# Scores of four attention layers from float32r parts instead of bf16 parts, with two heads on row tiles of the array

## The chip, the cores and the metric

The kernel runs on one core of one Trainium2 chip. The metric is the device time of one execution in microseconds, lower is better. Times of engines and queues come from one profiled execution.

## The reference, cut to what matters

Four layers follow each other on one batch of 2048 tokens of width 256. Each layer is a cross attention against a context of 1601 rows of width 192, and a mixture of experts:

```python
for L in range(4):
    x = x + xattn[L](layernorm(x), ctx_768)     # 2048 x 256 against 1601 x 192
    x = x + ffn[L](layernorm(x))                # 16, 8, 8, 16 experts

def xattn(x, y):                                # 16 heads of 16; layer 2: 8 heads of 32
    q, k, v = x @ Wq + bq, y @ Wk + bk, y @ Wv + bv
    att = softmax(q @ k.T / sqrt(dh))           # layer 3: masked keys, no biases
    return (att @ v) @ Wo + bo
```

All of it is float32. The softmax subtracts the exact maximum of each row.

## The kernel before, in words

The programs of the engines are written out by hand, one block an engine, with semaphores between them. Each layer has the stages normalisation, projections, attention, routing and experts, with a fence of all five engines between two stages. The change touches the first three.

**Normalisation.** Meanwhile POOL clears `v` and writes its columns of ones (L645, L646), then joins the fence. In layer 0 a fence stands ahead of this, which SP joins after it has issued the loads of `x`, the context, the mask (L410, L412, L414) and the weights.

**Projections.** 16 tiles of 128 x 512, first the keys and then the queries. TensorE forms a tile (L1476 to L1480), ScalarE copies it twice out of PSUM (`qk` as f32, `qk_part` as bf16, L771 and L773), VectorE forms the second and the third bf16 part of what is left (L1007 to L1009), and SP stores three parts to DRAM (L433). A head's product q k is then six products of parts. SP loads the keys back as `k_stack` (L371): six parts of 16 rows one below the other, 16 heads, all 1601 keys, and under them four constant rows (L360) for the mask and for the maximum. In layer 2 (heads of 32 rows) six parts don't fit in 96 rows, so each head has two such stacks (`nsub` = 2), and every score or maximum is two matmuls that accumulate.

**Attention.** Four iterations of 512 queries, each of four groups of 4 heads (layer 2: 2 heads), each group of 13 slots of 128 keys. Iterations 1 and 2 are a loop. In one slot TensorE issues, in this order:
- side jobs, taken from a list that `side_schedule` spreads over the 13 slots: two ahead of the scores, the others between them;
- `scores` of the slot for each head: keys as weights, 512 queries as the moving operand (L1566). Two heads fill a pair of banks; there are two pairs, banks 0 to 3;
- `weigh` of the slot before: v as weights of 32 (64) columns on a column tile for each head, the exponentials as moving operand, two instructions each, accumulated in bank 4 over the 13 slots (L1580).

ScalarE takes the exponential of a pair of banks in one instruction (L797), in layer 3 with the mask as bias. The side jobs use banks 5 to 7 in turn. TensorE waits for VectorE to have finished the job three back. The jobs are:
- `max`: 128 queries against 401 or 400 keys of a head of the next group, or the one after it (L1536), of which VectorE takes the row maximum (L1028). 64 of them make a group's maxima (layer 2: 32, each of two matmuls);
- `turn`: the maxima transposed (L1539), negated and split in three bf16 parts by VectorE (L1035 to L1040), stored and loaded as rows 97 to 99 of `q_stack` by SP (L399, L404). The scores of that group wait for them;
- `den`, `spread`: the denominators are picked out (L1542), inverted (L1046), widened by ScalarE, transposed (L1546), and applied by VectorE (L1051);
- `out`: four times in an iteration, eight f32 matmuls with Wo (L1551), added to x (L1057). All four fall in the first group.

In a prologue ahead of the loop, group 0 and three eighths of group 1 get their maxima, 88 jobs. SP loads the queries of the next groups (L384) as `weigh` frees their buffers.

TensorE's order within a slot, and the two waits that pace it:

```python
for job in slot[:2]: side(job)
for j in range(npair):
    for i in range(2):
        scores(g, k, j, i)          # i == 0 waits for the exponentials of two pairs back
        for job in slot[cut[2*j+i]:cut[2*j+i+1]]: side(job)   # waits for VectorE, three jobs back
weigh(g, k - 1)
```

## Time and profile before

| | |
|---|---|
| median of 3 runs (lowest, highest) | 4534.62 us (4534.21, 4538.73) |
| profiled execution: span from the first to the last instruction | 4547.7 us |
| instructions | 61161 |
| TensorE matmul busy | 3983.5 us, 88% |
| TensorE weight load busy | 1804.0 us, 40% |
| VectorE busy | 2670.7 us, 59% |
| ScalarE busy | 1975.0 us, 43% |
| GpSimd busy | 207.4 us, 5% |
| mean granted TensorE clock | 0.915 of full speed |

The page gives the span of the profiled execution and no other time for it. Busy time is the union of an engine's instructions. Matmuls overlap each other, so the mean duration of one is longer than the distance between two. PEld is TensorE's weight load, which runs beside its matmuls.

### The profile page before, as it was taken

How to read it: one execution, taken by the hardware profiler on the slowest of the kernel's cores; microseconds unless marked ns; L12 is line 12 of the kernel's file. 1: busy time of each engine (PE TensorE's matmuls, PEld its weight loads, DVE VectorE, ACT ScalarE, POOL GpSimd, SP SyncE). 2: the span in 40 equal slices, each digit the busy share in tenths (PEclk: the TensorE clock that was granted, in tenths of full speed). 3: DMA queues.
4: the chain of work that ended last, by engine and by line, in shares of the span. 5: the costliest groups of instructions: out<-in, count | busy, mean ns of one | idle time of the engine just before them, and what ended most of it. 6: DMA issues, size and time to landing. Idle time of an engine off the chain costs nothing. (4 is left out here: it accounts for less than half of the span.)

```text
span 4547.7 us, 61161 instructions
## 1 busy us (share of the span) xinstructions
PE 3983.5 (88%) x19174; PEld 1804.0 (40%) x19175; DVE 2670.7 (59%) x5907; ACT 1975.0 (43%) x2374; POOL 207.4 (5%) x420
## 2 busy tenths in 40 slices
PE   4999999699599999947994799999786999997894
PEld 2233333466323333335663234443441333333463
DVE  3888786445488878632224554443456887883322
ACT  2476677222247667712332243334012766765110
POOL 1000000000000000021003000000000000001202
PEclk8799999899779999958997899999795999997897
DMA  7000000000600000042113200000023000001144
GB/s 135 15 12 13 10 12 2 18 18 18 101 12 12 13 10 12 2 161 102 31 31 90 64 12 12 11 9 1 23 47 67 12 13 9 12 5 66 49 146 111
DMA packets 131231, 170.84 MB, mean 38 GB/s; under 512 B 30119, under 2 KB 111215, under 8 KB 128914
## 3 DMA queue, kind: packets, MB, share of 16 engines
q1 hardware_dynamic: 121362, 136.37, 12.2%
q0 software_dynamic: 9600, 31.04, 2.3%
q8 instruction: 149, 2.44, 0.2%
q14 instruction: 120, 0.98, 0.1%
HBM read 114.12 MB, written 54.66 MB: 37 GB/s over the span
## 5 line engine op out<-in xcount | busy, mean ns | idle before, releaser
L1028 DVE TENSOR_REDUCE mx<-ps 128x1 f32<-128x400 f32 (+1 forms) x3584 | 1809.8, 565 | 538.7 <-PE ps L1536 533.9
L797 ACT ACTIVATE probs<-ps,zero_col 128x1024 f32<-128x1024 f32 (+1 forms) x1040 | 1111.7, 1110 | 741.0 <-PE ps L1566 740.6
L1536 PE MATMUL ps<-k_stack,q_stack 97*128 97x400 bf16 (+3 forms) x4096 | 1233.1, 352 | 142.9 <-DMA q_stack<-ones_row 120.7
L1566 PE MATMUL ps<-q_stack,k_stack 100*128 100x512 bf16 (+2 forms) x3328 | 1080.9, 383 | 4.1 <-ACT probs L797 3.9
L1580 PE MATMUL ps<-probs,v 128*32 128x512 f32 (+2 forms) x5824 | 896.9, 611 | 0.2 <-ACT probs L797 0.2
L1536 PEld LDWEIGHTS ps<-k_stack,q_stack 97*128 97x128 bf16 (+1 forms) x4096 | 343.7, 98 | 1255.2 <-DVE mx L1028 703.6
L797 ACT ACTIVATE probs<-ps,mask_col 128x1024 f32<-128x1024 f32 (+1 forms) x416 | 440.3, 1110 | 188.1 <-PE ps L1566 187.9
L1566 PEld LDWEIGHTS ps<-q_stack,k_stack 100*128 100x128 bf16 (+2 forms) x3328 | 325.0, 100 | 321.5 <-ACT probs L797 59.1
L1283 DVE SCALAR_TENSOR_TENSOR x_res<-ps,comb,x_res 128x256 f32<-128x256 f32 x336 | 149.1, 483 | 154.5 <-PE ps L1710 154.1
L1580 PEld LDWEIGHTS ps<-probs,v 128*32 128x32 f32 (+2 forms) x5824 | 140.3, 112 | 234.1 <-issue 223.2
L1695 PE MATMUL ps<-xn_t,w_up 128*128 128x512 f32 (+1 forms) x416 | 192.8, 603 | 34.1 <-DVE comb L1182 22.6
L1448 PE MATMUL ps<-ident,xn 128*128 128x128 f32 x256 | 51.6, 383 | 146.7 <-DVE xn L984 109.5
L1710 PE MATMUL ps<-w_down,h_t 128*128 128x256 f32 x736 | 170.2, 380 | 4.0 <-ACT h_t L892 4.0
L1710 PEld LDWEIGHTS ps<-w_down,h_t 128*128 128x128 f32 x736 | 138.9, 190 | 53.5 <-issue 37.4
L1774 PE MATMUL ps<-w_all,xn_t 128*128 x624 | 144.6, 385 | 3.8 <-ACT xn_t L861 2.4
L1753 PE MATMUL ps<-w_all,xn_t 128*128 x312 | 142.4, 599 | 0.4 <-issue 0.4
L1007 DVE TENSOR_TENSOR qk_rest<-qk,qk_part 128x512 f32<-128x512 f32 x64 | 40.5, 633 | 172.0 <-ACT qk_part L771 128.4
L1551 PE MATMUL ps<-wo,o_t 128*128 128x256 f32 x512 | 131.1, 405 | 11.0 <-DVE mx L1028 7.6
L1774 PEld LDWEIGHTS ps<-w_all,xn_t 128*128 128x128 f32 x624 | 118.2, 192 | 43.0 <-issue 28.4
L861 ACT ACTIVATE xn_t<-ps,tile_bias 128x128 f32<-128x128 f32 x312 | 84.7, 382 | 99.7 <-PE ps L1765 99.4
L892 ACT ACTIVATE h_t<-ps 128x512 f32<-128x512 f32 x80 | 46.7, 596 | 177.0 <-PE ps L1695 176.9
L1695 PEld LDWEIGHTS ps<-xn_t,w_up 128*128 128x128 f32 (+1 forms) x416 | 79.6, 192 | 110.5 <-issue 95.1
(205 smaller groups left out, 2664.4 us busy)
## 6 DMA issues: line engine op xcount, KB each, us to landing
q_stack<-q_parts SPq DMA_DIRECT2D x384, 64.0 KB, 2.3
k_stack<-k_parts SPq DMA_DIRECT2D x48, 400.2 KB, 12.2
q_parts<-qk_part SPq DMA_DIRECT2D x32, 384.0 KB, 10.1
w_up<-in_up SPq DMA_DIRECT2D x17, 704.0 KB, 4.4
x_place<-zeros POOLq DMA_DIRECT2D x2, 5120.0 KB, 26.5
k_parts<-qk_part SPq DMA_DIRECT2D x24, 384.0 KB, 5.8
w_all<-in_up SPq DMA_DIRECT2D x5, 1024.0 KB, 16.4
w_all<-in_down SPq DMA_DIRECT2D x5, 1024.0 KB, 19.8
```

Source lines behind the costliest of these rows:

```text
L797: act.activation(PR[pair[0] % 4][0:r, :, :], PS[0:r, 2 * b:2 * b + 2, :], ACT.Exp, bias=mask_col[0:r, k:k + 1] if L == 3 else zero_col[0:r ...
L861: last = act.activation(HB[:, q * P:(q + 1) * P], PS[:, 2 + q // 4, q % 4 * P:(q % 4 + 1) * P], ACT.Gelu, bias=BT[:, bass.ds(i, 1), q], sc ...
L1028: ins = dve.reduce_max(MX4[g % 2][:, u, c:c + 1], PS[:, bank, 0:CK[c]], AX.X)
L1283: dve.scalar_tensor_tensor(X[:, t, :], PS[:, b, 0:D], c, X[:, t, :], ALU.mult, ALU.add).then_inc(s_yf, 1)
L1536: last = mm(PS[:, bank, 0:CK[c]], QS[g][0:rows, s, qt * P:(qt + 1) * P], KS[0:rows, ks0, CKO[c]:CKO[c] + CK[c]], start=sub == 0, stop=sub ...
L1551: last = mm(PS[:, bank, 0:D], OT[:, g, i * P:(i + 1) * P], WO[:, g, :], start=g == 0, stop=g == NG - 1)
L1566: last = mm(PS[0:r, b + i, :], KS[0:rows, (g * hpg + jj) * nsub + sub, k * P:k * P + r], QS[g][0:rows, slot_of(jj) + sub, :], start=sub == ...
L1580: last = mm(PS[pw * jj:pw * jj + pw, 4, :], V[0:r, k, (g * hpg + jj) * pw:(g * hpg + jj) * pw + pw], PR[used[0] % 4][0:r, i, :], start=k = ...
L1695: last = mm(PS[0:rows, b, :], up[:, k, off + at:off + at + rows], xnT[:, k, c * Q:(c + 1) * Q], start=k == 0, stop=k == 1)
L1710: last = mm(PS[:, b, 0:D], HT[(c - 1) % 2][0:rows, t, i * P:(i + 1) * P], WD[par][0:rows, t, :], start=t == 0, stop=t == len(ft) - 1)
L1753: last = mm(PS[:, half, :], XT1[par][:, k * P:(k + 1) * P], w1.rearrange("p a f -> p (a f)"), start=k == 0, stop=k == 1)
L1774: last = mm(PS[:, 4 + par, 0:D], HB[:, q * P:(q + 1) * P], w2.rearrange("p a f -> p (a f)"), start=q == 0, stop=q == NF // P - 1)
```

## The change

The six bf16 products become three products of float32r parts: q and k are each kept as two f32 words of which TensorE reads the leading part (float32r), stored in DRAM and in SBUF as 4 bytes. A head of 16 rows now takes 3 x 16 + 3 = 51 rows, so two heads stand one above the other, on rows 0 to 63 and 64 to 127 of the array (`hps` = 2); a head of 32 takes 99 rows in one piece (`hps` = 1, no second matmul). The mask goes in as a row of `k_stack` in layer 3, and the maximum as two rows. The constant rows come from clearing the whole of `k_stack` to 1 and of `q_stack` to 0 (1 in layer 3) on POOL, ahead of the fence that ends normalisation. A score tile is now one bank (banks 0 to 2 in turn) with an exponential of its own; the sums are in bank 3. A maximum job covers two heads, in two banks at a time (4 and 5, or 6 and 7), with one VectorE instruction for both; TensorE waits for the job two back. No side job stands ahead of a slot's first score any more. Matmuls of the maxima are issued so that the row halves alternate. The mask columns, their loads and the bias of the exponentials are gone.

```diff
-CK = [401, 400, 400, 400]
+CK = [402, 400, 400, 400]
-ATT = [dict(dh=16, pw=32, hpg=4, nsub=1), dict(dh=16, pw=32, hpg=4, nsub=1),
-       dict(dh=32, pw=64, hpg=2, nsub=2), dict(dh=16, pw=32, hpg=4, nsub=1)]
+ATT = [dict(dh=16, pw=32, hpg=4, hps=2), dict(dh=16, pw=32, hpg=4, hps=2),
+       dict(dh=32, pw=64, hpg=2, hps=1), dict(dh=16, pw=32, hpg=4, hps=2)]
+Q_PART, K_PART = [0, 0, 1], [0, 1, 0]
...
-    units = hpg * TPQ
+    units = hpg // 2 * TPQ
...
-    jobs = late + early[:6] + ([("turn", (g + 1) % NG)] if nxt1 else []) + early[6:]
+    jobs = late + early[:3] + ([("turn", (g + 1) % NG)] if nxt1 else []) + early[3:]
...
-            KS = sb("k_stack", [100, 16, S], bf16, att)
+            KS = sb("k_stack", [P, 8, S], f32r, att)
-            PR = [sb(f"probs{i}", [P, 2, Q], f32, att) for i in range(4)]
-            QS = [sb(f"q_stack{i}", [100, 4, Q], bf16, att) for i in range(4)]
+            QS = [sb(f"q_stack{i}", [P, 2, Q], f32r, att) for i in range(4)]
+            PR = [sb(f"probs{i}", [P, Q], f32, att) for i in range(8)]
...
-            QP = [sb(f"qk_part{i}", [P, 3, Q], bf16, prj) for i in range(4)]
+            QP = [sb(f"qk_part{i}", [P, 2, Q], f32r, prj) for i in range(4)]
...  SP
-                load_constant_rows(L)
+                if L == 3:
+                    load_mask_rows(L)
...
+                keys = k_parts[K_PART[third]].rearrange("(s i d) n -> i d s n", i=hps, d=dh)
+                for i in range(hps):
+                    row = 64 * i + third * dh
+                    sp.dma_start(KS[row:row + dh, half * 4:half * 4 + 4, :].bitcast(f32),
+                                 keys[i][:, half * 4:half * 4 + 4, :]).then_inc(s_ks, 16)
...
+                for third in range(3):
+                    queries = q_parts[Q_PART[third]].rearrange("(s i d) t -> i d s t", i=hps, d=dh)
+                    for i in range(hps):
+                        row = 64 * i + third * dh
+                        sp.dma_start(QS[buf][row:row + dh, :, :].bitcast(f32),
+                                     queries[i][:, 2 * g:2 * g + 2, bass.ts(c, Q)]).then_inc(s_ql[buf], 16)
-                sp.dma_start(dst[96:97, :, :], ones_row[:]).then_inc(s_ql[buf], 16)
...
-            sp.dma_start(mask_u8[:, 0:NK - 1], A["mask"][:, 0:P * (NK - 1)].rearrange("a (k p) -> p (a k)", p=P),
-                         allow_slow_non_contiguous=True).then_inc(s_in, 16)
-            sp.dma_start(mask_u8[0:KREM, NK - 1:NK], A["mask"][:, P * (NK - 1):S].rearrange("a p -> p a"),
-                         allow_slow_non_contiguous=True).then_inc(s_in, 16)
...  POOL
+                for buf in QS:
+                    link(pool.memset(buf[:].bitcast(f32), 1.0 if L == 3 else 0.0))
+                link(pool.memset(KS[:].bitcast(f32), 1.0))
                 fence(pool, fences)
-                link(pool.memset(MP[:, 0, :], 0.0))
...  ACT
-                    for j in range(npair):
-                        b = pair[0] % 2
+                    for j in range(hpg):
                         sc.step()
                         act.wait_ge(s_sc, sc.at())
-                        if pv.n > 3:
-                            act.wait_ge(s_pv, pv.at(3))
-                        pv.step()
-                        act.activation(PR[pair[0] % 4][0:r, :, :], PS[0:r, 2 * b:2 * b + 2, :], ACT.Exp,
-                                       bias=mask_col[0:r, k:k + 1] if L == 3 else zero_col[0:r, :],
-                                       scale=1.0).then_inc(s_pr, 1)
+                        if j % 2 == 0:
+                            if pv.n > 3:
+                                act.wait_ge(s_pv, pv.at(3))
+                            pv.step()
+                        act.activation(PR[tile[0] % 8][0:r, :], PS[0:r, tile[0] % 3, :], ACT.Exp).then_inc(s_pr, 1)
...  DVE
-                    link(dve.tensor_tensor(r, x, p[:, 0, 0:n], ALU.subtract))
-                    link(dve.tensor_copy(p[:, 1, 0:n], r))
-                    dve.tensor_tensor(p[:, 2, 0:n], r, p[:, 1, 0:n], ALU.subtract).then_inc(s_pp, 1)
+                    dve.tensor_tensor(p[:, 1, 0:n], x, p[:, 0, 0:n].bitcast(f32), ALU.subtract).then_inc(s_pp, 1)
...
-                    bank = 5 + njob[0] % 3
+                    bank = 4 + 2 * (njob[0] % 2)
...
-                        ins = dve.reduce_max(MX4[g % 2][:, u, c:c + 1], PS[:, bank, 0:CK[c]], AX.X)
+                        lo = u // TPQ * 2 * TPQ + u % TPQ
+                        dve.reduce_max(MX4[g % 2][:, lo:lo + TPQ + 1:TPQ, c], PS[:, bank:bank + 2, 0:CK[c]], AX.X)\
+                            .then_inc(s_sf, 1)
...
-                        link(dve.tensor_copy(MP[0:units, 1, :], neg))
-                        link(dve.tensor_tensor(rest, neg, MP[0:units, 1, :], ALU.subtract))
-                        link(dve.tensor_copy(MP[0:units, 2, :], rest))
-                        dve.tensor_tensor(MP[0:units, 3, :], rest, MP[0:units, 2, :], ALU.subtract).then_inc(s_mp, 1)
+                        link(dve.tensor_copy(MP[0:units, 0, :], neg))
+                        dve.tensor_tensor(MP[0:units, 1, :], neg, MP[0:units, 0, :].bitcast(f32), ALU.subtract)\
+                            .then_inc(s_mp, 1)
...  PE
+                def place_of(j):
+                    return 64 * (j % hps), j // hps
...
-                        if sf.n > 2:
-                            pe.wait_ge(s_sf, sf.at(2))
+                        if sf.n > 1:
+                            pe.wait_ge(s_sf, sf.at(1))
...
-                        for sub in range(nsub):
-                            rows = 97 if sub == 0 else 96
-                            s = slot_of(j) + sub
-                            ks0 = (g * hpg + j) * nsub + sub
-                            last = mm(PS[:, bank, 0:CK[c]], QS[g][0:rows, s, qt * P:(qt + 1) * P],
-                                      KS[0:rows, ks0, CKO[c]:CKO[c] + CK[c]], start=sub == 0, stop=sub == nsub - 1)
+                        for i in (high, 1 - high):
+                            row, s = place_of(u // TPQ * 2 + i)
+                            end = row + 3 * dh + 1
+                            last = mm(PS[:, bank + i, 0:CK[c]], QS[g][row:end, s, qt * P:(qt + 1) * P],
+                                      KS[row:end, 2 * g + s, CKO[c]:CKO[c] + CK[c]], start=True, stop=True)
...
+                def scores(g, k, j):
                     r = key_rows(k)
+                    if tile[0] == 0:
+                        if pr.n > 0:
+                            pe.wait_ge(s_pr, pr.at())
+                    elif tile[0] > 2:
+                        pe.wait_ge(s_pr, pr.at(2))
+                    pr.step()
+                    row, s = place_of(j)
+                    end = row + 3 * dh + 3
+                    mm(PS[0:r, tile[0] % 3, :], KS[row:end, 2 * g + s, k * P:k * P + r], QS[g][row:end, s, :],
+                       start=True, stop=True).then_inc(s_sc, 1)
+                    tile[0] += 1
...
-                            for job in slot[:2]:
-                                side(job)
-                            cut = [2 + n for n in chunk_of(max(len(slot) - 2, 0), 2 * npair)]
-                            for j in range(npair):
-                                for i in range(2):
-                                    scores(g, k, j, i)
-                                    for job in slot[cut[2 * j + i]:cut[2 * j + i + 1]]:
-                                        side(job)
+                            cut = chunk_of(len(slot), hpg)
+                            for j in range(hpg):
+                                scores(g, k, j)
+                                for job in slot[cut[j]:cut[j + 1]]:
+                                    side(job, 1 - j % 2)
```

## Rows read from the trace of the kernel before

**Rows 1.** Windows: prologue and main loop of layer 0, main loop of layer 2.
```profile
core 0: us, PE busy (x) PEld busy (x) DVE busy (x) ACT busy (x) POOL busy (x), PEclk, DMA share, GB/s
114.70:160.60 45.90, 42.64 (x91) 9.50 (x92) 43.97 (x95) 0.00 (x0) 0.00 (x0) 0.50 0.10 26
160.60:802.00 641.40, 632.22 (x3693) 223.02 (x3692) 511.03 (x1080) 452.10 (x443) 0.00 (x0) 0.99 0.03 9
...
2541.00:3168.00 627.00, 623.06 (x2909) 243.87 (x2910) 306.56 (x637) 245.85 (x237) 0.00 (x0) 0.99 0.03 10
```

**Rows 2.** Timeline, a slot of layer 3: start, length, engine, line, count, wait.
```profile
3560.30 1.07 PE L1580 MATMUL ps<-probs,v 128*32 128x512 f32 x8
...
3561.30 0.51 PE L1536 MATMUL ps<-k_stack,q_stack 97*128 97x400 bf16 x2
...
3561.64 0.60 PE L1566 MATMUL ps<-q_stack,k_stack 100*128 100x512 bf16 x2
3561.68 2.50 DVE L1028 TENSOR_REDUCE mx<-ps 128x1 f32<-128x400 f32 x5 [0.33 <-PE ps L1536]
...
3562.08 0.33 PE L1536 MATMUL ps<-k_stack,q_stack 97*128 97x400 bf16 x1
...
3562.28 2.12 ACT L797 ACTIVATE probs<-ps,mask_col 128x1024 f32<-128x1024 f32 x2 [0.71 <-PE ps L1566]
...
3563.12 1.07 PE L1580 MATMUL ps<-probs,v 128*32 128x512 f32 x8
```

**Rows 3.** Chain of waits, layer 3: start, length, what.
```profile
3454.38 30.90 DVE mx L1028 x64
...
3547.24 1.03 PE ps L1542 x8
...
3586.34 1.02 PE ps L1542 x8
...
3677.85 1.91 PE ps L1551 x8
...
3827.47 1.86 PE ps L1580 x8
...
3850.03 1.92 PE ps L1551 x8
...
4015.14 1.97 PE ps L1551 x8
```

**Rows 4.** Timeline, layer 2, two successive `weigh` blocks.
```profile
2602.96 1.08 PE L1580 MATMUL ps<-probs,v 128*64 128x512 f32 x4
...
2605.63 1.08 PE L1580 MATMUL ps<-probs,v 128*64 128x512 f32 x4
```

**Rows 5.** Groups by form: count, busy us, mean ns, idle before.
```profile
L1028 DVE TENSOR_REDUCE mx<-ps 128x1 f32<-128x400 f32 x2688 | 1408.8, 565 | 362.4 <-PE ps L1536 360.4
...
L1695 PE MATMUL ps<-xn_t,w_up 128*128 128x512 f32 x384 | 179.3, 604 | 34.1 <-DVE comb L1182 22.6 <-DVEq L1227 11.4
...
L1331 DVE COPY xn_t<-ps 128x512 f32<-128x512 f32 x78 | 53.9, 691 | 94.0 <-PE ps L1753 94.0
...
L741 ACT ACTIVATE xn_t<-ps 128x512 f32<-128x512 f32 x64 | 34.5, 596 | 79.3 <-PE ps L1448 79.2
...
L1339 DVE COPY xn_t<-ps 128x256 f32<-128x256 f32 x39 | 16.6, 424 | 119.4 <-PE ps L1774 119.4
```

**Rows 6.** Timeline, end of layer 1's loop, ScalarE back to back.
```profile
1931.51 4.16 ACT L797 ACTIVATE probs<-ps,zero_col 128x1024 f32<-128x1024 f32 x4 [0.19 <-PE ps L1566]
```

**Rows 7.** Timeline of POOL, normalisation of layer 1.
```profile
1153.94 5.64 POOL L645 MEMSET v<- 128x6656 f32 x1 [317.04 <-SPq L318]
...
1169.96 0.19 POOL L648 MEMSET m_part<- 16x128 bf16 x1 [9.87 <-ACTq L318]
```

**Rows 8.** Timeline of SP's queue at the start.
```profile
4.59 3.66 SPq L412 DMA_DIRECT2D mask_u<-in_mask  x1
```

**Rows 9.** Windows of the projections of layer 1, columns as in rows 1.
```profile
1172.00:1176.00 4.00, 4.00 (x14) 2.46 (x13) 2.12 (x4) 2.72 (x6) 0.00 (x0) 1.00 0.88 26
...
1236.00:1240.00 4.00, 0.00 (x0) 0.00 (x0) 0.83 (x2) 1.26 (x2) 0.00 (x0) 0.50 0.94 324
```

More of the change, by code:

```diff
@@ L831, in _ @@
                     n = NG * NK * npair
[L832 removed]
+                    for c, per in ((sc, 2 * n), (pv, n), (o, n), (ot, NG), (rd, NG), (dv, NG)):
                         c.loop(it, 1, per)
@@ L1079, in _ @@
                 with dve.Fori(1, NQ - 1) as it:
-                    loops = ((sj, per), (sf, per), (md, 64), (v, 4 * 3), (rx, NG))
+                    loops = ((sj, per), (sf, per), (md, 64), (v, 4), (rx, NG))
                     for c, p in loops:
@@ L1553, in side @@
                     last.then_inc(s_sj, 1)
-                def scores(g, k, j, i):
+                def scores(g, k, j):
                     r = key_rows(k)
-                    b = 2 * (pair[0] % 2)
-                    if i == 0:
-                        if pr.n > 1:
-                            pe.wait_ge(s_pr, pr.at(1))
-                        pr.step()
-                    jj = 2 * j + i
-                    for sub in range(nsub):
-                        rows = 100 if sub == 0 else 96
-                        last = mm(PS[0:r, b + i, :], KS[0:rows, (g * hpg + jj) * nsub + sub, k * P:k * P + r],
-                                  QS[g][0:rows, slot_of(jj) + sub, :], start=sub == 0, stop=sub == nsub - 1)
-                    if i == 1:
-                        pair[0] += 1
-                        last.then_inc(s_sc, 1)
+                    if tile[0] == 0:
[8 more added lines that the diff above has]
+                       start=True, stop=True).then_inc(s_sc, 1)
+                    tile[0] += 1
                 def weigh(g, k):
```

137 lines of the change are left out of this document (51 added, 86 removed).

## The prediction

> **What bounds the kernel now.** I looked first at the windows of the stages [rows 1]. The main loop of attention in layer 0 takes 641 us and that of layer 2 627 us; layers 1 and 3 run the loop of layer 0 again, so four such loops are over half of the 4547.7 us span. TensorE is busy for 632 of the 641 us at clock 0.99, VectorE for 511, ScalarE for 452. A busy engine need not be the limit, so the timeline of one key slot comes next [rows 2]. From one start of the eight `weigh` matmuls (L1580) to the next it is 2.82 us (3560.30 to 3563.12), and TensorE has no hole in it: `weigh` 1.00 us, then five maxima matmuls (L1536) 0.17 us apart (two of them from 3561.30 to 3561.64) and four score matmuls (L1566) 0.22 us apart (two from 3561.64 to 3562.08), 5 x 0.17 + 4 x 0.22 = 1.73 us, and about 0.1 us where the kind of matmul changes. VectorE's five maxima take 2.50 us, ScalarE's two exponentials 2.12 us. TensorE ends last, VectorE 0.3 us behind it. The chain of waits [rows 3] gives the pace of a whole group (13 slots, 64 maxima): the eight `den` matmuls (L1542) are 39.1 us apart, 13 x 2.82 = 36.7 plus den, spread and turn. An iteration of four groups is 172.2 or 165.1 us from `out` to `out` (L1551), so the group that holds the four `out` jobs is 48 to 55 us; I take 51. Layer 2 has half the exponentials and is bound by TensorE alone: 2.67 us between its `weigh` blocks [rows 4].
>
> **TensorE, layers 0, 1 and 3.** Matmuls per slot stay at 4 scores and 64/13 = 4.92 maxima, each now on 51 or fewer rows of one half of the array, the halves alternating. No row shows float32r or two row halves at work together. Bounds: at best two at a time at today's column rate, 1.71 / 2 = 0.85 us per slot; at worst no overlap, 1.71 us. (4 x 0.215 + 4.92 x 0.172 = 1.71.) What may come between is the weight load, since four-byte weights load slower: the `den` matmuls, four columns behind 128 f32 weights each, are 1.03 / 8 = 0.129 us apart [rows 3]. 8.92 x 0.129 = 1.15 us. I take 1.15, because the `weigh` matmuls, eight f32 ones on four column tiles, already finish in 1.00 us, where eight on the whole array at 0.467 us (L1695, 179.3 us busy for 384 [rows 5]) would take 3.7: this array does overlap tiles. With 1.00 for `weigh` and 0.1 for the changes of kind a slot is 2.25 us of TensorE, a group 29.3 + 2 (den, spread, turn) = 31.2, the `out` group 7.7 more (4 x 1.92 [rows 3]) = 38.9.
> The row shows 0.1 us per slot lost between kinds of matmul, no more [rows 2]. The Trainium skill ("TensorEngine Tiling (Array Packing)", Tiling Modes) says that a change of tiling mode drains the engine. By that rule den, spread, turn and out, which now stand between row-tiled matmuls, would add some ten changes a group, 1 us; it would alter only the `out` groups, by 10 us in all.
>
> **VectorE.** 64 maxima of 400 columns become 32 of 800. 64 of them back to back take 30.90 us in the prologue, 0.483 us each [rows 3], against a duration of 0.565 [rows 5]. A copy goes from 0.424 to 0.691 us for 256 columns more [rows 5], 1.04 ns a column. So 800 columns cost 0.483 + 400 x 1.04 ns = 0.90 us; the bounds are 0.90 and 2 x 0.483 = 0.97. A group is 32 x 0.90 = 28.8 us, and the other jobs (reciprocal, spread, turn, final reduce with their waits for TensorE) about 3.3: 32.1 us. VectorE becomes the bound of an ordinary group. 33 jobs over 13 slots are six slots of two and seven of three. In a slot of two VectorE needs 1.8 us and TensorE 8 x 0.129 + 1.1 = 2.1, so 6 x 0.3 = 1.8 us may be lost, with two pairs of banks where three single ones stood: 32.1 to 33.9 us, and I take 33.5. The `out` group stays with TensorE: 38.9 plus the 3 us by which today's exceeds its own sum (36.7 + 2 + 7.7 = 46.4 against 48 to 55), 42 us.
>
> **ScalarE.** Two activations of 1024 columns become four of 512. Four of the long ones back to back take 4.16 us [rows 6], 1.02 apart against a duration of 1.11; a short one lasts 0.60 [rows 5], so 0.51 apart: 2.04 us a slot both ways. If the 0.09 us did not overlap it would be 2.4, still under 2.58 (33.5 / 13). Cost nothing while VectorE covers it. A score waits for the exponential three tiles back, and three tiles are 1.5 us of ScalarE's work against 1.0 us of `weigh`.
>
> **Sum for layers 0, 1, 3.** Of 16 groups 11 are ordinary and full, 11 x (39.1 - 33.5) = 62 us; three have `out`, 3 x (51 - 42) = 27, of which I count 24; one has five eighths of the maxima (4); the last has none and is ScalarE's (1). 91 us a layer, **-273**.
>
> **Layer 2.** 99 rows hold all three products, so scores fall from 4 to 2 matmuls a slot and maxima from 4.92 to 2.46, untiled. 1.71 becomes 0.85 us if float32r streams as bf16 does, and TensorE stays the bound (VectorE 1.23 x 0.90 + 0.25 = 1.4, ScalarE 1.0). 0.85 x 13 = 11 us a group, some 170 us; I take off 20 for an overhead per four-byte matmul like that of L1695 (0.467 us against twice the 0.213 us that 512 columns take at 2.4 GHz: 0.04): **-150**.
>
> **The rest.** The prologue is VectorE's: 44 x 0.90 = 39.6 against 88 x 0.483 = 42.5, -3 a layer, **-12**. The two new clears on POOL, 4 x 1024 columns of `q_stack` and 12808 of `k_stack`, stand before the fence that ends normalisation. `v`'s 6656 columns take 5.64 us [rows 7], so they cost 14.9 us. POOL now ends 9.9 us before that fence (L645, L646, then idle until 1169.96), so the fence comes 5 us later in each layer. In layer 0 the longer of the two removed mask loads gives SP 3.7 us back ahead of the first fence [rows 8], leaving 1. Together **+17**. In the projections the four constant rows go, whose broadcasts keep the DMA engines 0.88 busy at only 26 GB/s as the projections begin [rows 9], some 5 us, and the stored parts grow from 384 to 512 KB a tile, 1.8 MB a layer, 5.5 us at the 324 GB/s at which the last stores drain [rows 9]. I count **0**, with 10 us a layer either way. TensorE now has pauses, and its clock may fall at times, as it is 0.50 in the prologue, where it waits for VectorE [rows 1]. I add **+25**.
>
> -273 - 150 - 12 + 17 + 25 = -393 us from the 4547.7 us span: 4155. The page gives no other time for that execution; the median of the runs, 4534.6, is 13.1 us less than its span, so the forecast is **4142 us**. Its own range is 4050 to 4250: 32.1 us a group is -55, 35 us +60, the projections and clears 40 either way.
>
> **Rivals.** (1) *The halves do not overlap*, or the waits between them keep them apart. TensorE's slot stays 2.82 us, and only layer 2 gains (and no pauses cost clock): 4547.7 - 150 - 12 + 17 - 13 = **4390**. For it: nothing here shows row tiles. Against: column tiles overlap. Chance 0.13.
> (2) *The clock falls*, the case that ends slower. It decides in the main loops of layers 0, 1, 3, where TensorE would wait for VectorE some 0.3 us of each slot. At 0.5 clock `weigh` takes 1.86 us [rows 3] and the pairs 1.67 by columns, 3.7 us a slot, 1.15 more than my 2.58. Over 46 groups that is 690 us if it lasts, and it outweighs the gain from 57% of the time on; at all times about 4830. At 30% of the time it is 4350. For it: the prologue runs at 0.50 with TensorE shown busy for 42.6 of 45.9 us [rows 1]. Against: at half clock TensorE has no pause, and today that brings the clock back as soon as the main loop starts. 0.06 for a part of it, 0.04 for slower.
> (3) *float32r takes the passes of f32.* f32 needs two instructions of 0.467 us for 512 columns [rows 5]. Overlapped in pairs, layers 0, 1, 3: (4 x 0.93 + 4.92 x 0.73) / 2 + 1.1 = 4.8 us a slot; layer 2 the same without overlap: about 6000 us. With one such instruction instead of two the slot is 2.9 everywhere, some 80 us slower than before. 0.05 together.
> (4) *The parts hold up but VectorE gains nothing* (0.97 a job, all coupling lost): 36.5 us a group, 4240. Within 0.72 for the forecast.
>
> **Numbers.** Forecast and (4) 0.72, (1) 0.13, part of (2) 0.06, slower 0.09. A measurement of this kernel tells about 0.2%, 9 us, from no change. Faster 0.90, same 0.01, slower 0.09. The range 4050 to 4395 takes in (1) and most of (2).
>
> **What would show it.** L1028 at half the count and 0.97 to 1.0 us each; den to den 33 to 34 us in layer 3; alternate L1566-like matmuls starting 0.13 us apart or less; VectorE's waits for TensorE small and TensorE's for VectorE large; layer 2's slot near 2.0 us with two score matmuls 0.22 us apart; the fence after normalisation 5 us later; granted clock above 0.95 in all four main loops. Wrong: matmuls in alternate halves 0.2 us apart, a float32r duration near 0.6 us, or clock 0.5 inside the loops.

## The result: slower by 6%, and the profile after

The changed kernel takes 4811.5 us (median of four runs, 4792.3 to 4842.8) against 4535.9 us before (4534.2 to 4538.7), a ratio of 1.0616 with an interval of 1.0571 to 1.0661. The forecast was 4142 us. The profiled execution has a span of 4840.7 us, 293 us over the one of before. From its page: the span, the busy times, and the granted clock in 40 slices.

```profile
span 4840.7 us, 58262 instructions
...
PE 4026.7 (83%) x18246; PEld 2014.0 (42%) x18247; DVE 2522.0 (52%) x3854; ACT 1953.7 (40%) x3830; POOL 262.3 (5%) x434
...
PEclk8698888699969989965998698888885988995797
```

The windows of attention in the four layers, each from its first exponential to its last, before and then after (the columns as in [rows 1], whose windows are cut a little otherwise):

```profile
163.10:806.30 643.20, 633.87 (x3712) 222.98 (x3710) 509.18 (x1077) 454.97 (x446) 0.00 (x0) 0.99 0.03 9
1297.20:1940.00 642.80, 633.49 (x3712) 222.81 (x3710) 509.46 (x1077) 455.04 (x446) 0.00 (x0) 0.99 0.04 9
2557.60:3171.60 614.00, 612.86 (x2876) 239.82 (x2873) 293.89 (x609) 246.81 (x239) 0.00 (x0) 1.00 0.03 9
3502.20:4146.70 644.50, 634.97 (x3712) 223.16 (x3710) 509.49 (x1077) 455.20 (x447) 0.00 (x0) 0.99 0.04 9
```
```profile
163.90:911.60 747.70, 689.02 (x3707) 283.82 (x3710) 481.59 (x582) 447.11 (x862) 0.00 (x0) 0.86 0.03 8
1414.80:2148.60 733.80, 671.42 (x3707) 275.12 (x3710) 481.47 (x582) 447.25 (x862) 0.00 (x0) 0.88 0.03 8
2775.80:3356.70 580.90, 544.07 (x2003) 260.02 (x2002) 265.19 (x350) 248.41 (x447) 0.00 (x0) 0.87 0.03 9
3687.20:4435.50 748.30, 690.43 (x3709) 281.93 (x3710) 481.70 (x582) 447.59 (x863) 0.00 (x0) 0.86 0.03 8
```

Layers 0, 1 and 3 lose 105, 91 and 104 us, and layer 2 gains 33. That is +267 of the 293 us. Two things changed: TensorE had at most 10 us of holes in a layer and now has 37 to 62 us, and its granted clock fell from 0.99 to between 0.86 and 0.88. The costliest groups by line say what ends the holes (busy time and mean ns of one, then idle time before them and what ended it):

```profile
L1005 DVE TENSOR_REDUCE mx<-ps 128x2 f32<-128x800 f32 (+1 forms) x1792 | 1710.0, 988 | 832.1 <-PE ps L1511 827.5
L782 ACT ACTIVATE probs<-ps 128x512 f32<-128x512 f32 (+1 forms) x2912 | 1527.9, 600 | 1175.4 <-PE ps L1541 1168.5 <-issue 5.4
...
L1511 PEld LDWEIGHTS ps<-k_stack,q_stack 49*128 49x128 f32 (+1 forms) x3584 | 518.2, 214 | 378.5 <-DVE mx L1005 236.1 <-issue 122.0 <-DVE m_neg L1012 0.9
L1541 PEld LDWEIGHTS ps<-q_stack,k_stack 51*128 51x128 f32 (+2 forms) x2912 | 462.8, 204 | 1222.8 <-ACT probs L782 752.4 <-issue 402.9 <-DMA q_stack<-m_parts 39.1
```

VectorE and ScalarE wait for TensorE, and TensorE's weight loads wait for both of them: a ring, in which no engine is full. The timeline of one slot of layer 1 at granted clock 1.00 shows it (start, duration, engine and line, and in brackets the idle time and its releaser):

```profile
1530.15 0.50 PE L1541 MATMUL ps<-q_stack,k_stack 51*128 51x512 f32 x2
...
1530.66 0.40 PE L1541 MATMUL ps<-q_stack,k_stack 51*128 51x512 f32 x1
1530.68 2.06 ACT L782 ACTIVATE probs<-ps 128x512 f32<-128x512 f32 x4 [1.08 <-PE ps L1541]
1530.87 1.00 DVE L1005 TENSOR_REDUCE mx<-ps 128x2 f32<-128x804 f32 x1 [0.50 <-PE ps L1511]
...
1531.33 0.49 PE L1541 MATMUL ps<-q_stack,k_stack 51*128 51x512 f32 x1 [0.27 <-ACT probs L782]
...
1531.33 0.67 PE L1511 MATMUL ps<-k_stack,q_stack 49*128 49x400 f32 x2
...
1531.93 1.06 PE L1553 MATMUL ps<-probs,v 128*32 128x512 f32 x8
1532.04 0.99 DVE L1005 TENSOR_REDUCE mx<-ps 128x2 f32<-128x800 f32 x1 [0.17 <-PE ps L1511]
...
1532.93 0.50 PE L1541 MATMUL ps<-q_stack,k_stack 51*128 51x512 f32 x2
...
1533.46 1.58 ACT L782 ACTIVATE probs<-ps 128x512 f32<-128x512 f32 x3 [0.71 <-PE ps L1541]
```

The two scores at 1530.15 start and end together, 0.50 us for both, where two took 0.60 us before [rows 2]: the halves do overlap. But the fourth score finds all three score banks taken and waits for the first exponential (1530.68 + 0.60). `weigh` stands behind that score, and ScalarE, done at 1532.74, gets its next tile only 0.5 us after `weigh` ends. In series: score 0.5, exponential 0.6, fourth score and maxima 0.6, `weigh` 1.0, some 2.8 us (here 2.78; more in a slot of three maxima jobs). The mean slot at clock 1.00 is 3.12 us, against 2.93 before, both counted as said below.

### The profile page after: what moved, and what is told of

Read it like the earlier page. It is cut to its first block and busy times, and to the rows that moved or that the text cites. A ratio compares the mean times of both kernels' runs of the same rounds, so it can differ in the third digit from the quotient of the medians.

```text
span 4840.7 us, 58262 instructions
## 1 busy us (share of the span) xinstructions
PE 4026.7 (83%) x18246; PEld 2014.0 (42%) x18247; DVE 2522.0 (52%) x3854; ACT 1953.7 (40%) x3830; POOL 262.3 (5%) x434
## 5 line engine op out<-in xcount | busy, mean ns | idle before, releaser
L1005 DVE TENSOR_REDUCE mx<-ps 128x2 f32<-128x800 f32 (+1 forms) x1792 | 1710.0, 988 | 832.1 <-PE ps L1511 827.5
L782 ACT ACTIVATE probs<-ps 128x512 f32<-128x512 f32 (+1 forms) x2912 | 1527.9, 600 | 1175.4 <-PE ps L1541 1168.5
L1541 PE MATMUL ps<-q_stack,k_stack 51*128 51x512 f32 (+2 forms) x2912 | 1146.7, 517 | 147.6 <-ACT probs L782 94.0
L1511 PE MATMUL ps<-k_stack,q_stack 49*128 49x400 f32 (+3 forms) x3584 | 924.1, 428 | 191.3 <-DMA q_stack<-q_parts 115.9
L1553 PE MATMUL ps<-probs,v 128*32 128x512 f32 (+2 forms) x5824 | 1033.6, 699 | 0.0
L1541 PEld LDWEIGHTS ps<-q_stack,k_stack 51*128 51x128 f32 (+2 forms) x2912 | 462.8, 204 | 1222.8 <-ACT probs L782 752.4
L1511 PEld LDWEIGHTS ps<-k_stack,q_stack 49*128 49x128 f32 (+1 forms) x3584 | 518.2, 214 | 378.5 <-DVE mx L1005 236.1
L985 DVE TENSOR_TENSOR qk_part<-qk,qk_part 128x512 fp32r<-128x512 f32 x64 | 39.9, 633 | 232.3 <-ACT qk_part L757 162.4
L1424 PEld LDWEIGHTS ps<-ident,xn 128*128 128x128 f32 x256 | 49.7, 218 | 196.1 <-issue 102.9
```

The lines of the kernel that those rows point to most:

```text
L782: act.activation(PR[tile[0] % 8][0:r, :], PS[0:r, tile[0] % 3, :], ACT.Exp).then_inc(s_pr, 1)
L1005: dve.reduce_max(MX4[g % 2][:, lo:lo + TPQ + 1:TPQ, c], PS[:, bank:bank + 2, 0:CK[c]], AX.X)\
L1424: last = pe.transpose(PS[:, 2 * (c % 2) + half, i * P:(i + 1) * P], XN[:, c * TPQ + i, half * P:(half + 1) * P], ident[:])
L1511: last = mm(PS[:, bank + i, 0:CK[c]], QS[g][row:end, s, qt * P:(qt + 1) * P], KS[row:end, 2 * g + s, CKO[c]:CKO[c] + CK[c]], start=True, s ...
L1541: mm(PS[0:r, tile[0] % 3, :], KS[row:end, 2 * g + s, k * P:k * P + r], QS[g][row:end, s, :], start=True, stop=True).then_inc(s_sc, 1)
L1553: last = mm(PS[pw * jj:pw * jj + pw, 3, :], V[0:r, k, (g * hpg + jj) * pw:(g * hpg + jj) * pw + pw], PR[used[0] % 8][0:r, :], start=k == 0 ...
```

## The experiments

"A slot" below is the mean distance from the first exponential of one slot to that of the next, in layers 0, 1 and 3, over the slots that run at clock 1.00 from end to end, without the groups that hold the `out` jobs. Each comes from the run's one profiled execution. The edits are cut to the lines that matter.

### The order in the changed kernel

**e1_weigh_before_last.** In slots of four heads, `weigh` goes ahead of the last score.
```diff
-    for j in range(hpg): scores(g, k, j); ...
-    weigh(g, k - 1)
+    for j in range(hpg):
+        if j == hpg - 1 and hpg == 4: weigh(g, k - 1)
+        scores(g, k, j); ...
```


> The changed kernel, but in the layers with four heads a group TensorE issues the weigh matmuls ahead of the slot's last score instead of behind it. Theory chain: with three score banks the last score of a slot waits for the exponential of the slot's first score, and weigh stands behind it, so score latency 0.5, exponential 0.6, last score and maxima 0.6 and weigh 1.0 follow one another (2.8 to 3.0 us a slot at full clock). With weigh moved ahead of that wait the slot falls to 2.4 to 2.6 us, den to den in layers 1 and 3 at full clock from 41 to 33 to 36 us, and the total to 4250 to 4450 us, the clock rising above 0.93 as TensorE has fewer holes. Rival clock: the loss is the lower clock alone, set by what the matmuls are (half of the rows), so the slot at full clock changes little and the total stays within 1.5% of the changed kernel's 4812. Rival no overlap: the row halves do not work together and TensorE's own work fills the slot: no change beyond 1%.

4718.1 us, ratio 1.0398 (1.0362 to 1.0433), 94 us less. The exponential's wait is real, and a third of the loss. The slot falls from 3.12 to 2.98 us only, not to the 2.4 to 2.6 expected, so something else holds it as well.

**e3_same_half.** The second maximum of a pair no longer starts in the half that the last score left free.
```diff
-    side(job, 1 - j % 2)
+    side(job, j % 2)
```


> The changed kernel with the order of each maxima pair turned round, so that a maxima matmul follows a score on the same row half instead of the other one. If halves overlap, the matmuls that follow on the same half are 0.17 to 0.22 us apart and those that change half 0.10 to 0.13. Theory chain: in total under 1.5% slower, since the slot's length is waits. Rival no overlap: no difference in the distances at all.

4839.7 us in one run at clock 0.843, slot 3.11 us: no difference from the changed kernel that one run can tell.

**e4_half_maxima.** The maxima read 200 of each 400 columns; the rest is left out.
```diff
-    PS[:, bank:bank + 2, 0:CK[c]]
+    PS[:, bank:bank + 2, 0:CK[c] // 2]
```


> The changed kernel, but VectorE's maxima read half of the columns of each bank (the other half of the keys is left out of the maxima), so one lasts about 0.57 us instead of 0.99. Theory chain: VectorE is not what the slot waits for, the total falls by less than 2% (some 0.1 us a slot where a maxima pair waits for it). Rival VectorE with only two pairs of banks as the bound: the slot falls by about 0.4 us per job, 0.5 to 1 us a slot, 300 us or more in total.

4541.4 us in one run, 270 less, at clock 0.879, slot 2.93 us. That was far more than the theory of an exponential chain alone allowed: the wait for VectorE is the larger one.

**e6_early_weigh_half_maxima.** Both edits.

> The changed kernel with the weigh ahead of the last score (e1) and maxima that read half of their columns (e4); the other half of the columns is left out of the maxima. Theory (two waits in series in each slot, VectorE's and the exponential's): the gains add, -94 and -270 us on 4811, about 4450 us, and a slot at full clock is 2.3 to 2.4 us. Rival (one wait only, each edit shortens the same one): no better than e4 alone, 4520 to 4560 us, slot 2.6 us.

4437.0 us in one run: 374 less, where the two alone gave 94 and 270. The slot adds up too, 0.31 us less where the two alone gave 0.14 and 0.19, so the two waits lie in series. But it is 2.81 us, not the 2.3 to 2.4 expected.

### The banks, and what TensorE needs by itself

**e2_banks_as_before.** float32r parts and row tiles, but with the banks of before: two pairs of score banks, exponentials of 1024 columns, three banks for maxima of one head.
```diff
-    act.activation(PR[t % 8], PS[0:r, t % 3, :], ACT.Exp)
+    act.activation(PR[t % 4], PS[0:r, 2 * b:2 * b + 2, :], ACT.Exp)
-    dve.reduce_max(MX4[...], PS[:, bank:bank + 2, 0:CK[c]], AX.X)
+    dve.reduce_max(MX4[...], PS[:, bank, 0:CK[c]], AX.X)
```


> float32r parts and row tiles kept, but banks, activations and maxima jobs as in the kernel before: two pairs of score banks with one activation of 1024 columns, sums in bank 4, maxima one head at a time in banks 5 to 7. Theory chain: the two pairs of banks let scores run ahead through weigh again, so the slot is set by VectorE (4.92 x 0.483 plus 0.25 = 2.6 us) and the total is 4250 to 4400. Rival clock or no overlap: the slot in layers 0, 1, 3 stays at 2.8 or above and the total at 4450 or above, with only layer 2 gaining.

4756.3 us, ratio 1.0477 (1.0459 to 1.0495). **e7_half_maxima_old_banks** is the same with maxima of half their columns (the rest is left out).

> The kernel of e2_banks_as_before with maxima that read half of their columns (the other half is left out). With the old banks TensorE has 13 x 2.25 us of its own work in a group by the prediction and VectorE half of what it had. If TensorE's own work was priced rightly (2.25 us) and only waits for VectorE and the clock stood in the way: slots of 2.2 to 2.4 us at full clock and 4250 to 4400 us. If the pairs of halves with one head's maxima at a time do not overlap much, slots stay at 2.6 to 2.8 us and the time at 4600 to 4750 us.

4305.5 us in one run. The windows from 240 us of e2, and then of e7:

```profile
240.00:280.00 40.00, 38.51 (x234) 16.25 (x233) 33.47 (x70) 26.98 (x28) 0.00 (x0) 1.00 0.04 12
280.00:320.00 40.00, 39.10 (x216) 16.66 (x215) 30.64 (x65) 25.08 (x26) 0.00 (x0) 0.87 0.04 11
320.00:360.00 40.00, 39.50 (x191) 17.88 (x191) 28.04 (x59) 22.89 (x24) 0.00 (x0) 0.74 0.04 12
```
```profile
240.00:280.00 40.00, 39.88 (x269) 18.56 (x268) 24.41 (x79) 29.54 (x32) 0.00 (x0) 1.00 0.04 11
```

With VectorE out of the way TensorE is busy for 39.9 of 40 us, and its own slot is 2.63 us with the `den`, `spread` and `turn` jobs in it (forecast 31.2 / 13 = 2.40, before 2.93); the clock is 1.00 here and 0.97 to 0.98 over the loops. With the full maxima the slot is 2.88 us, and the clock doesn't stay: 0.87, 0.74. VectorE is busy for 33.5 of the 40 us and yet sets the pace. Rows of e2 say why:

```profile
244.97 2.50 DVE L1005 TENSOR_REDUCE mx<-ps 128x1 f32<-128x400 f32 x5 [0.46 <-PE ps L1511]
...
246.45 1.07 PE L1554 MATMUL ps<-probs,v 128*32 128x512 f32 x8
...
247.44 0.45 PE L1511 MATMUL ps<-k_stack,q_stack 49*128 49x400 f32 x2
...
247.92 2.01 DVE L1005 TENSOR_REDUCE mx<-ps 128x1 f32<-128x400 f32 x4 [0.45 <-PE ps L1511]
```

`weigh` holds TensorE from 246.45 to 247.44. VectorE has worked off its full banks by 247.47, and the next maximum comes out of TensorE only 0.45 us later. So a slot is some 2.4 us of VectorE's work (4.92 maxima, of which this one has five) and 0.45 us of hunger. This chain is read from the trace; no run here removed the hunger alone.

**e13_weigh_in_two_parts** was to take that hunger away: two heads of `weigh` after the second score, two at the end of the slot.
```diff
     for j in range(hpg):
         scores(g, k, j)
+        if j == 1: weigh(g, k - 1, [0])
-    weigh(g, k - 1)
+    weigh(g, k - 1, [1])
```


> e2_banks_as_before, but in layers 0, 1 and 3 the weigh of four heads (1.07 us in one piece, during which VectorE is out of scores: it waits 0.46 us in each slot) is done in two parts, two heads after the second score and two at the end of the slot. Theory (the slot in e2 is VectorE's 2.50 us and its 0.46 us of wait): VectorE's wait is at most 0.1 us, the slot 2.55 to 2.65 us at full clock, loops of 620 to 680 us as the clock allows, and the time 4500 to 4640 us. Rival (TensorE's own work and the exponentials' wait set the slot; VectorE's wait moves elsewhere): 4700 to 4780 us.

4871.2 us, ratio 1.0728, slower than e2, and both theories missed. The timeline of e13:

```profile
245.07 1.05 PE L1554 MATMUL ps<-probs,v 128*32 128x512 f32 x4
...
246.68 1.05 PE L1554 MATMUL ps<-probs,v 128*32 128x512 f32 x4
```

Four matmuls of `weigh`, on two column tiles, take the 1.05 us that eight on four tiles take (1.07 in [rows 2]): half as many heads save nothing. Each slot pays `weigh` twice. **e14_two_parts_one_score_twice** (e13 with the edit of e11 below) tells the rest:

> e13 with e11's second score twice. Theory: if e13's VectorE is then the bound at 2.5 to 2.6 us and TensorE still waits for it at 2.45 us of its own, the extra 0.13 us fills its gaps: clock 0.97 to 1.00 and 4420 to 4520 us, under the kernel before. Rival (TensorE is already the bound in e13): longer than e13 by 0.13 x 624 = 80 us.

5002.7 us, ratio 1.1000: 131 us over e13 for one more score in each of 624 slots, 0.21 us each, and the slot goes from 3.49 to 3.70 us. In e13 TensorE is the bound at clock 0.99, and an extra score is paid in full.

### What lowers the clock

**e5_zeros_all_rows.** e2, with four slots in `q_stack`, one per head, and zeros in the other head's rows. Nothing is tiled, so nothing overlaps.
```diff
-    mm(PS[...], KS[row:end, 2 * g + s, ...], QS[g][row:end, s, :])
+    mm(PS[...], KS[0:115, 2 * g + s, ...], QS[g][0:115, j, :])
```


> The kernel of e2_banks_as_before (float32r parts, old banks, exponentials and maxima), but in layers 0, 1 and 3 no matmul works on one half of the rows: q_stack holds four slots, one a head, with zeros in the other head's rows, and each score reads all rows 0 to 114 and each maximum 0 to 112, at the same 4 and 5.7 matmuls a slot. Nothing overlaps, so TensorE's work per slot goes back to what it was before: 32 maxima by 0.17 us and 13 slots of four 0.22 us scores and 1.0 us of weigh. Theory (the clock falls because half the rows stand still while TensorE shows itself busy): the granted clock is back at 0.97 to 1.0 in the loops of layers 0, 1 and 3, slots are 2.8 to 3.0 us, each loop 650 to 690 us against some 735 to 750, and the whole is 4560 to 4640 us, faster than e2 although it overlaps nothing. Rival (the clock falls at the waits for banks, whatever the rows hold): the clock stays near 0.85 and the time is that of e2 or above, 4750 to 4850 us.

4637.8 us, ratio 1.0190 (1.0173 to 1.0207): 118 us under e2, with matmuls that no longer overlap (slot 3.09 us for 2.88). Its window:

```profile
240.00:280.00 40.00, 40.00 (x228) 23.42 (x225) 32.67 (x68) 25.27 (x27) 0.00 (x0) 1.00 0.04 11
```

The number came as the theory of idle rows had it, but e7, half rows and clock 1.00, speaks against that theory. What e5 and e7 share is a TensorE busy for 39.9 to 40.0 of the 40 us, where e2 has 38.5. To tell gaps from rows, TensorE's gaps were filled on half rows, with nothing taken away: **e11_one_score_twice**, and **e12_two_scores_twice** (in the second pair too).
```diff
+    if hps == 2 and j == 0:          # e12: j in (0, 2)
+        mm(PS[0:r, b + 1, :], ...)   # the score of head j + 1, ahead of its turn
     last = mm(PS[0:r, b + j % 2, :], ...)
```


> e2_banks_as_before, but in layers 0, 1 and 3 the second score of each slot is computed twice, the first time ahead of the first score, which it overlaps: 0.13 us more for TensorE in each slot, and the same result. Theory (TensorE's gaps at its waits for VectorE lower the clock; e7 had no gaps and had 1.00 on half rows): TensorE's work comes nearer to VectorE's 2.5 us and 0.46 us of wait at the weigh, the gaps shrink, clock in the loops 0.90 to 0.95 and time 4600 to 4720 us, under e2's 4756. Rival (the clock falls with how many rows or tiles are at work, not with gaps): clock as in e2, 0.83 to 0.88, and 4760 to 4850 us.

> e11 with the fourth score twice as well: 0.26 us more for TensorE in each slot than e2. Theory (gaps lower the clock): the gaps are filled, clock in the loops 0.95 to 1.00 and the slot 2.75 to 2.9 us at full clock, 4500 to 4620 us, under e11. Rival: more work at the same clock, 4800 to 4950 us.

e11 4632.4 us (ratio 1.0205, 1.0179 to 1.0230), e12 4626.0 us (1.0186, 1.0169 to 1.0203). The window of e11:

```profile
240.00:280.00 40.00, 39.55 (x250) 17.52 (x246) 33.46 (x71) 26.23 (x29) 0.00 (x0) 1.00 0.04 12
```

An extra matmul per slot saves 124 us. At clock 1.00 the slot is even a little longer than e2's (2.95 us for 2.88), but the loops of layers 0, 1 and 3 now have 0.95 to 0.97 where e2 has 0.83 to 0.88. e12 stands level with e11 (their intervals overlap), just above what was expected. The traces of the profiled executions, layers 0, 1 and 3 together (1750 to 2270 us), say how TensorE's holes and the clock go together:

| run | slot, us | TensorE idle while its clock is 1.00 | time at clock 0.50, us |
|---|---|---|---|
| before | 2.93 | 1.5% | 42 |
| changed kernel | 3.12 | 10.0% | 598 |
| e1, weigh earlier | 2.98 | 6.8% | 478 |
| e4, half maxima | 2.93 | 7.7% | 232 |
| e6, both | 2.81 | 3.7% | 145 |
| e2, old banks | 2.88 | 4.1% | 601 |
| e11, one score twice | 2.95 | 2.0% | 150 |
| e12, two scores twice | 3.01 | 1.3% | 119 |
| e7, old banks, half maxima | 2.63 | 1.1% | 83 |
| e5, all rows | 3.09 | 0.6% | 9 |
| e13, weigh in two parts | 3.49 | 0.7% | 44 |

Every form without holes keeps the clock, on half rows too (e7, e13). e13 has e2's matmuls on e2's rows, in a slot 0.6 us longer, so neither resting rows nor fewer matmuls per microsecond lower the clock by themselves; and filling e2's holes brings it back (e11). But the size of the holes alone does not order the kernels: e4 has nearly twice the holes of e2 and spent 232 us at 0.50 against 601. What else decides is open.

**e9_high_maxima_all_rows** and **e10_one_score_more** mixed e2 and e5 to place TensorE's work between them: maxima of upper heads on all rows, and in e10 one score of four as well.
```diff
-    mm(PS[:, bank, ...], QS[g][row:end, j, ...], KS[row:end, ...])
+    mm(PS[:, bank, ...], QS[g][0 if i else row:end, j, ...], KS[0 if i else row:end, ...])
```


> e2_banks_as_before and e5_zeros_all_rows mixed: q_stack has four slots with zeros in the other head's rows as in e5, scores read their own half of the rows (and overlap), and of the maxima those of a head in the upper half read rows 0 to 112, so that no two maxima overlap. TensorE's slot by e5's 2.85 us at full clock less four scores' overlap (4 x 0.09) is 2.5 us; VectorE's own work in a slot is 4.92 maxima by 0.485 us at full clock and 0.1 for the rest, 2.5 us. Theory (the clock falls when TensorE waits for VectorE, whatever rows it reads, and e5 had the clock back because its TensorE work is longer than VectorE's): the two are level here, so some waits and some dips stay: clock 0.88 to 0.90, 4450 to 4600 us. Rival (rows that stand still lower the clock; e7 kept it for another reason): half of the matmuls read half of the rows, clock 0.86 to 0.88, 4650 to 4750 us.

> e9 with the second score of each slot on all rows too, so that one pair of scores overlaps and one doesn't: about 0.15 us more of TensorE's work in a slot, 2.65 us, against VectorE's 2.5 us. Theory (waits of TensorE lower the clock): TensorE waits less than in e9, the granted clock of the loops is nearer 1.00, and with a slot of 2.65 us at full clock, 13 x 16 x 3 slots, the kernel takes 624 x 0.2 = 125 us less than e5: about 4510 us; if e9's clock falls, e10 is the faster of the two although it has more work. Rival (rows): clock between e9's and e5's, time between e9's 4650 to 4750 and e5's 4638 us.

The fastest of e9's four runs took 5175.2 us and the others up to 5409.6, too far apart for a ratio; e10 took 6406.6 us, ratio 1.398. Neither theory had foretold this. Two windows of e9, and matmuls of it in between:

```profile
200.00:240.00 40.00, 40.00 (x118) 14.13 (x119) 19.41 (x38) 14.27 (x14) 0.00 (x0) 0.50 0.00 1
840.00:880.00 40.00, 40.00 (x205) 16.57 (x203) 31.52 (x64) 24.66 (x26) 0.00 (x0) 1.00 0.04 12
```
```profile
206.75 0.29 PEld L1514 LDWEIGHTS ps<-k_stack,q_stack 113*128 113x128 f32 x1 [0.56 <-issue]
...
207.38 0.28 PEld L1545 LDWEIGHTS ps<-q_stack,k_stack 51*128 51x128 f32 x1 [0.34 <-issue]
```

At each change between all rows and half of them the next weight load comes 0.34 to 0.56 us after the end of the last one (at half clock), with no semaphore to wait for: it starts only as the matmul before it ends. The slot is 3.30 us at clock 1.00, where the sum gave 2.5. The Trainium skill ("TensorEngine Tiling (Array Packing)", Tiling Modes) says that changing the tiling mode drains the engine; these rows agree. And the clock stays at 0.50 for stretches of nearly 200 us although TensorE shows 40.00 busy of 40: a busy PE in such a row doesn't show the drains. That they lower the clock as the waits do is argued from e9 and e10, not shown by an edit of its own.

### Layer 2

In 300 us of the changed kernel's layer 2 (from 2800 us), TensorE's scores have these waits:

```profile
PE ps L1541 <- DMA q_stack<-m_parts: 19.0, 8, 3.1
```

The change counts jobs in pairs, and `units * 3 // 8`, 3 of 8 before, is 1 of 4 in layer 2; the turn, from which the next group's m rows are made, comes after 15 of 16 jobs, where it came after 26 of 32. **e16_turn_earlier_in_layer_2** puts it after 13 of 16, in layer 2 alone.
```diff
-    jobs = late + early[:3] + [turn] + early[3:]
+    n = 3 if hpg == 4 else 1
+    jobs = late + early[:n] + [turn] + early[n:]
```


> The changed kernel with one number of its schedule put back in proportion: in layer 2 the turn (from whose maxima the subtracted rows of the next group are made and sent through memory) comes after 13 of 16 jobs, as in the kernel before (26 of 32), where the change made it 15 of 16; layers 0, 1 and 3 are untouched. Theory (layer 2 waits for its m rows, 19.0 us in 300 us of the changed kernel's layer 2, and its clock falls with that wait; e15, with the turn at 26 of 32, took 485 us for the loop against the changed kernel's 585): the waits on q_stack<-m_parts vanish, the granted clock of the loop goes from 0.87 to 0.93 or more, the loop takes 500 to 540 us, and the whole 4730 to 4770 us. Rival (e15's 485 us come from its banks and its 1024-wide exponentials, the wait is only moved to another one): the loop stays at 570 to 585 us and the whole at 4790 to 4830 us.

4733.8 us, ratio 1.0400 (1.0348 to 1.0452), 78 less. Its layer 2, from the first to the last exponential:

```profile
2750.70:3231.80 481.10, 476.51 (x2003) 232.01 (x2002) 264.59 (x350) 247.64 (x447) 0.00 (x0) 0.99 0.04 11
```

That is 481 us where the changed kernel took 581, and the clock is 0.99 for 0.87. The waits for the m rows, some 2 us a group and 32.5 us in all, are gone; the time at clock 0.50 in layer 2 fell with them from 153 to 5 us, and that makes up most of the rest.

**e15_layer_2_alone.** The kernel before, with float32r parts in layer 2 only, where one head's three products fill 99 rows without tiles; its banks, schedule and maxima stay.
```diff
+    if L == 2:
+        last = mm(PS[0:r, b + i, :], KSR[0:99, 2 * g + jj, ...], QSR[g][0:99, jj, :],
+                  start=True, stop=True)
-    for sub in range(nsub):
+    for sub in range(0 if L == 2 else nsub):
```


> The kernel before in layers 0, 1 and 3, with two float32r parts in three products in layer 2 alone (one matmul per score and maximum on 97 or 99 rows where before had two on 96 and 97 to 100; banks, maxima and exponentials as before; no row tiles). Theory (where one head fills the rows the three products halve TensorE's work of scores and maxima, and nothing else binds): layer 2's loop takes 560 to 585 us where before took 627, its prologue is 5 us shorter, and clearing k_stack in layer 2 costs 5 to 12 us; 4475 to 4510 us, under the kernel before by 30 to 60 us. Rival (waits and clock dips in the other loops come from layer 2's new form too, or the clear eats the gain): 4530 to 4560 us.

**4433.2 us (4426.1 to 4438.0), ratio 0.9715 (0.9701 to 0.9729): faster than both kernels**, 128 us under the kernel before where 30 to 60 were expected. Its layer 2 takes 476 us against 614:

```profile
2561.20:3036.80 475.60, 473.77 (x1996) 226.53 (x1994) 275.51 (x579) 246.65 (x238) 0.00 (x0) 1.00 0.04 11
```

### The clears

**e8_clear_on_scalar.** ScalarE clears five of the eight parts of `k_stack`, GpSimd three.
```diff
-    pool.memset(KS[:], 1.0)
+    pool.memset(KS[:, 5:8, :], 1.0)
+    for i in range(5): act.activation(KS[:, i, :], C0[:], ACT.Copy, scale=0.0, bias=1.0)
```


> The changed kernel, but five of the eight parts of k_stack are cleared by ScalarE, in its idle time ahead of the square root, and three by GpSimd. Theory (GpSimd's 10.8 us clear runs beside VectorE's 16 normalisations and doubles each, 0.41 to 1.08 us, and delays the fence): the 16 take 6 to 8 us where they took 17.35, the fence of layers 1 to 3 comes 8 to 12 us earlier, and the whole is 20 to 40 us under the changed kernel's. Rival (the normalisations wait for TensorE and are hidden): no change in the fence.

The timelines of normalisation ahead of layer 1, in the kernel before, in the changed kernel and then in e8. The first row of each is the statistics, and the last the first matmul behind the fence (before, the fence falls at 1169.96 [rows 7]):

```profile
1153.98 5.33 DVE L972 BATCH_NORM_STATS2 stat<-x_res 128x6 f32<-128x256 f32 x16
...
1161.29 5.25 DVE L984 TENSOR_SCALAR xn<-x_res,mv,rstd 128x256 f32<-128x256 f32 x16
```
```profile
1266.87 5.32 DVE L950 BATCH_NORM_STATS2 stat<-x_res 128x6 f32<-128x256 f32 x16
...
1274.59 17.35 DVE L962 TENSOR_SCALAR xn<-x_res,mv,rstd 128x256 f32<-128x256 f32 x16
1277.12 10.80 POOL L633 MEMSET k_stack<- 128x12808 f32 x1
...
1295.76 1.12 PE L1455 MATMUL ps<-ctx_a,wk 128*128 128x512 f32 x2 [1.21 <-ACTq L315]
```
```profile
1243.41 5.33 DVE L952 BATCH_NORM_STATS2 stat<-x_res 128x6 f32<-128x256 f32 x16
...
1252.53 9.90 DVE L964 TENSOR_SCALAR xn<-x_res,mv,rstd 128x256 f32<-128x256 f32 x16
1253.64 4.13 POOL L633 MEMSET k_stack<- 128x4803 f32 x1
...
1265.95 1.12 PE L1457 MATMUL ps<-ctx_a,wk 128*128 128x512 f32 x2 [1.32 <-ACTq L315]
```

Sixteen operations of 0.40 us take 17.35 us, for one of them lasts 10.9 us, as long as the clear. In e8 the longest lasts 4.3 us, beside a clear of 4.1, and the sixteen take 9.90 us, not the 6 to 8 expected. From the first statistics to the fence it was 16.0 us before, is 28.9 in the changed kernel and 22.5 in e8. The whole, 4834.1 us in one run, doesn't show the 19 us of three layers; the changed kernel's own four runs lie 50 us apart.

## Why the prediction was wrong

**What held.** float32r streams at one pass, two half-row scores run side by side, and TensorE's own slot falls: 2.63 us measured (e7) for 2.40 forecast. VectorE's paired maxima cost what was forecast: 30 of them back to back in the prologue start 0.90 us apart. Rivals (1), (3) and (4) fall.

**Where the time went.** For layers 0, 1 and 3 the forecast was -273 us and the trace shows +300: some 110 us are the longer slot (3.25 us for 3.07 at clock 1.00 with the `out` groups in, 624 times) and the other 190 the granted clock. For layer 2 it was -150, and the trace shows -33. The rest was to cost 5 us and cost 26.

**The step that failed first** was "Cost nothing while VectorE covers it. A score waits for the exponential three tiles back, and three tiles are 1.5 us of ScalarE's work against 1.0 us of `weigh`". That compares amounts of work, but the fourth score stands in TensorE's queue ahead of `weigh`: it waits for an exponential that could only start when the slot's first score was done. ScalarE's idle time was not cover, it was the other side of the same wait: 94 us (e1).

**The larger one** was the sum for VectorE, "6 x 0.3 = 1.8 us may be lost" in a group. The 33.5 us a group, 2.58 us a slot, added up its jobs as if a bank were always full; the slot is 3.12 us. In each slot `weigh` holds TensorE for 1.0 us, longer than the banks last, and VectorE then waits, 0.45 us with the old banks (e2), 13 times a group: 5.9 us. The row for it was there: in [rows 2] VectorE stands idle for 0.33 us until the first maximum behind `weigh`, and 0.33 + 2.50 us of its maxima is the slot of 2.82 us. The prediction read that as VectorE ending 0.3 us behind TensorE, and took the time as TensorE's alone. Halving VectorE's work took 270 us off the changed kernel (e4) and 451 us off the one with the old banks (e7).

**The clock** was rival (2), with 0.10 of the chance, and +25 us in the sum, a term that measured some 190. Its place was right, and its reason too as far as e11 shows it (TensorE has holes inside the loop). Its price was right as well: layers 0, 1 and 3 spent 598 of 2230 us at 0.50, or 27%, for which rival (2) asks 0.27 x 690 = 186 us, and slots at 0.50 took 4.56 us, 1.3 more than at 1.00, where it had 1.15. It needed no 57% of the time to end slower, because the gain that it was to outweigh was not there. "At half clock TensorE has no pause" was wrong: at 0.50 TensorE still stands idle for 0.26 us ahead of the fourth score of a slot (at 872.65 us), and a fall lasted 18 us on average.

**Layer 2** was priced at -150 us and gained 33. The term was right: e15 gives 138 us. What failed is an edit that the forecast passed over, the turn that moved from 26 of 32 to 15 of 16 (e16).

**The clears** were to put the fence 5 us later and put it 12.9 us later ahead of layer 1. POOL's own time was forecast rightly, 14.9 us for 14.8 measured (though by the rate of [rows 7] the sum gives 14.3, and 3 x 5 + 1 is 16, not 17). What was missed is that VectorE stands still beside the clear of `k_stack`, which [rows 7], with its clear of 5.64 us ahead of the normalisations, could not show.

One term leaned the forecast too low by itself: today's `out` group exceeds its own sum by 51 - 46.4 = 4.6 us, and 3 were carried over, 14 us in all.

## What to carry to other kernels

Work in a slot adds up to a bound only if every queue has something at every moment: for each engine, look at the longest stretch in which the engine ahead of it does something else, and at how many buffers cover it. A wait written ahead of another engine's food turns spare time into part of the ring. And where TensorE is nearly full, a change that makes it wait a little costs twice, once by the wait and once by the clock; the cheapest cure measured here was a useless matmul in the gap, and the best version kept the new parts only in layer 2, where they leave no gap.

## What the runs showed of the hardware

- An extra matmul per slot raised the granted clock of the loops, 0.83 to 0.88 without it, to between 0.95 and 0.97 and saved 124 us of 4756 (e2, e11).
- The same matmuls on the same half rows, in a slot of 3.49 us without holes: clock 0.99 (e13). The size of the holes does not order the clocks of different forms (e2, e4).
- Matmuls that alternate between all rows and half of them: 5175 and 6407 us where either form alone took 4638 and 4756, at clock 0.50 for long stretches with TensorE shown 100% busy (e9, e10).
- Two float32r scores on the two row halves start and end together, 0.50 us for both (changed kernel).
- `weigh` on two column tiles takes 1.05 us, on four 1.06 (e13, changed kernel).
- VectorE's 0.40 us operation lasted 10.9 us beside GpSimd's 10.8 us clear (changed kernel, e8).
